# Eight of sixteen gate tiles of a Mamba input projection move into the scan

## Chip, cores and metric

The kernel runs on one core of a Trainium2 chip. The metric is the device time of one execution in microseconds (us), lower is better. Engines are named as the profile names them: PE is the matrix engine, PEld its weight load, DVE the vector engine, ACT the scalar engine, POOL the GpSimd engine, SP the sync engine, which here only issues DMAs. An "ACTq" or "SPq" row is a DMA issued by that engine.

## The reference

One decoder layer on x of shape 2 x 512 x 1024: a Mamba block, a cross attention and a feed-forward, each followed by a residual add and a layer norm. Only the Mamba block is touched by the change:

```
proj = x @ in_proj_w                       # 1024 -> 4096
x, z = split(proj)                         # 2048 channels each; z is the gate
xc   = silu(causal_conv4(x))
dt_r, B, C = rmsnorm of the parts of x_proj(xc)   # 64, 16, 16
dt   = softplus(dt_r @ dt_proj_w.T + dt_bias)
h    = exp(dt * A) * h + dt * B * xc       # per channel and state, 16 states
y    = (sum over states of h * C + D * xc) * silu(z)
out  = y @ out_proj_w.T
```

## The kernel before

The layer is five phases, one after the other. Each phase has its own buffers and semaphores, and the next phase starts when the last has finished. The change touches the first three.

**The input phase** (`mamba_in`, L100) works on tiles of 128 output channels of the projection, for both batch items at once (1024 columns). Tiles 0 to 15 are x, 16 to 31 are z. One tile (`main`, L426) is 8 blocks of the contraction x 2 batch items x 3 passes (`three_passes`, L93: weights and data are split into a high and a low fp32r part, and three products give fp32 accuracy) = 48 matmuls of 512 columns. ACT makes the high part of the next weight tile (L254) and DVE the low part (L332). For an x tile ACT copies the result out (L279), DVE does the four-tap convolution (L358, L363), ACT applies Silu (L281) and PE adds the tile's share of x_proj. The convolved x (`xc`) stays in SBUF for all 32 pairs of tile and batch item, through the scan. For a z tile ACT applies Silu on the way out of PSUM (`gate`, L264) and SP stores it to the DRAM tensor `sz`.

After z tile 17 the 96 rows of x_proj are normalised: PE means (L460), ACT root (L294), DVE reciprocal (L372) and scale (L374, which signals `n_done`). Then the step size dt is made for the 16 channel tiles, two at a time ("a pair"): PE `dt_products` (L470, fp32), ACT Abs and Relu (L302, L303), Exp (L306), Ln (L311), DVE the rest of the softplus (L382, L385, L389, L392, which signals `dt_done`), POOL u = dt * xc (L422). ACT begins a pair's Abs only when DVE has ended the pair before (L298). The loops of L214, L313, L394 and L473 put one pair beside two z tiles, so seven rounds and a tail hold the 14 z tiles from 18 on and eight pairs. SP issues everything in program order: weight load, gate store, weight load, two small dt weight loads, gate store, two dt stores, two u stores (L214 to L226).

**The scan phase** (`mamba_scan`, L483) has 32 blocks (16 channel tiles x 2 batch items), each of NK = 8 steps of two states. Step n of the sequence is

```
POOL dbx(n)  = u * B                        (L732)  128 x 1024
ACT  exp(n)  = exp(dt * A), into PSUM       (L673)  two of 128 x 512
DVE  scan(n), in place in PSUM              (L711)  two of 128 x 512
DVE  g(n-1)  = state * C, PSUM to SBUF      (L701)  128 x 1024
PE   sum(n-1): identity x g, into ps_y      (L758)  two fp32 matmuls
```

The states lie in three PSUM slots (`ps_a`), so exp(n) waits for g(n-3). DVE runs scan(n) half 0, scan(n) half 1, g(n-1). The g buffers are three too, so g(n) waits for sum(n-3). At the start of a block PE adds D * xc with a diagonal matrix (L754) into `ps_y`, for which ACT must have copied out the block before (`after`, L663, placed ahead of the exps of step 4). In blocks 1 to 24, PE also computes the keys of the cross attention with plain fp32 matmuls: 8 chunks of three blocks ("tiles" 0, 1, 2); per block 4 products before the diagonal one and two after each of the steps 0 and 1. ACT copies them out and issues their store at the end of the block, behind the exps of step 7 and ahead of the next block's (`store_keys`, L650). SP brings dt and u two blocks ahead, B and C broadcast to all partitions at the start and at block 16, and the context chunks (L589).

**The output phase** (`project_norm_qkv`, L903) multiplies y by the stored gate on POOL (L1207), splits the product and the output weights into high and low parts (ACT L1066, L1068, DVE L1150, L1152) and runs 32 steps of 24 three-pass products. Three DMAs feed each step: y, gate, weights.

## Time and profile before

| what | us |
|---|---|
| median of 3 runs | 3653.8 |
| lowest, highest | 3651.33, 3656.36 |
| span of the profiled execution | 3652.9 |
| input phase, first instruction to last gate copy | 0 to 424 |
| scan, first DVE scan to last g | 446 to 1309 |
| output phase, the 32 steps | 1326 to 1509 |
| mean granted PE clock, as a share of full speed | 0.972 |

The device time printed for the profiled execution is its span, from the first to the last instruction. Over the whole span the page gives PE 88% busy, DVE 62%, ACT 42%, POOL 34%. Those shares are averages over phases with different limits; each phase is read by itself. A fp32 matmul of 512 columns shows as two records, each with its own PEld record, a fp32r one shows as one.

### The profile page before, as it was taken

The page shows a single profiled execution, that of the slowest core. Times are in us where ns is not written, and L with a number is a line of the kernel's source. Part 1 is how long each engine was busy: PE and PEld are TensorE (multiplying, and loading weights), DVE is VectorE, ACT ScalarE, POOL GpSimd, SP SyncE. Part 2 cuts the span into 40 slices and gives each one's busy share as a digit, 9 for nine tenths or more (in the row PEclk, how much of TensorE's full clock was granted, in tenths as well). Part 3 has the DMA queues.
Part 4 walks back from the last instruction along what each step waited for, and adds up shares of the span by engine and source line. Part 5 has one row for each costly group of instructions (what it writes and reads, how often), then busy time and mean ns, then how long its engine had stood idle before and what let it go on. Part 6 is the DMA issues. An engine that isn't in the chain of part 4 may idle for free. (4 is left out here: it accounts for less than half of the span.)

```text
span 3652.9 us, 41367 instructions
## 1 busy us (share of the span) xinstructions
PE 3225.7 (88%) x12763; PEld 2382.3 (65%) x12763; DVE 2268.0 (62%) x1989; ACT 1518.3 (42%) x2148; POOL 1255.7 (34%) x730
## 2 busy tenths in 40 slices
PE   9999677777776679999799999997889999999996
PEld 7877433333332247888577777776768888888884
DVE  6544499999999956630277777775553233333326
ACT  4457544444444423321177888784231121121111
POOL 0002377667777732100077777772000000000001
PEclk9999799999999999999899999999999999999998
DMA  2124621113111046432211111114211111111101
GB/s 108 40 93 146 223 95 49 45 49 134 45 49 42 20 155 248 158 103 78 93 31 32 33 31 35 31 32 178 93 56 58 35 57 46 40 57 52 36 27 58
DMA packets 125431, 273.18 MB, mean 75 GB/s; under 512 B 24448, under 2 KB 38656, under 8 KB 122400
## 3 DMA queue, kind: packets, MB, share of 16 engines
q1 hardware_dynamic: 107632, 262.42, 21.1%
q10 hardware_dynamic: 17712, 9.79, 0.9%
q8 instruction: 32, 0.52, 0.1%
q14 instruction: 55, 0.45, 0.0%
HBM read 207.87 MB, written 64.29 MB: 75 GB/s over the span
## 5 line engine op out<-in xcount | busy, mean ns | idle before, releaser
L732 POOL TENSOR_TENSOR scan_dbx<-scan_u,scan_b_bc 128x1024 f32<-128x1024 f32 x256 | 602.6, 2355 | 278.4 <-DVE scan_ps_a L711 246.5
L758 PE MATMUL scan_ps_y<-scan_g,scan_ident 128*128 128x512 f32 x1024 | 505.3, 620 | 190.0 <-DVE scan_g L701 190.0
L711 DVE TENSOR_TENSOR_SCAN scan_ps_a<-scan_ps_a,scan_dbx 128x512 f32<-128x512 f32 x512 | 597.0, 1212 | 20.0 <-POOL scan_dbx L732 20.0
L1508 POOL TENSOR_TENSOR at_p_lo<-at_p,at_p_hi 128x512 fp32r<-128x512 f32 x384 | 513.2, 1344 | 176.3 <-ACT at_p_hi L1416 164.0
L673 ACT ACTIVATE scan_ps_a<-scan_dt,scan_a_neg 128x512 f32<-128x512 f32 x512 | 332.8, 682 | 497.4 <-DVE scan_g L701 497.4
L758 PEld LDWEIGHTS scan_ps_y<-scan_g,scan_ident 128*128 128x128 f32 x1024 | 185.7, 194 | 479.7 <-DVE scan_g L701 324.1
L886 POOL TENSOR_TENSOR ff_y<-ff_y,ff_rstd 128x512 f32<-128x512 f32 x14 | 24.9, 1805 | 1126.6 <-DVE ff_rstd L875 1126.6
L1454 DVE TENSOR_REDUCE at_neg_max<-at_ps_mx 128x1 fp32r<-128x1536 f32 x132 | 231.9, 1757 | 174.9 <-PE at_ps_mx L1528 162.4
L701 DVE TENSOR_TENSOR scan_g<-scan_ps_a,scan_c_bc 128x1024 f32<-128x1024 f32 x256 | 308.8, 1207 | 0.0
L1413 ACT ACTIVATE at_p<-at_ps_s 128x512 f32<-128x512 f32 x384 | 228.1, 594 | 116.2 <-PE at_ps_s L1545 96.3
L1928 DVE TENSOR_TENSOR ff_hf<-ff_sg,ff_ps_u 128x1024 f32<-128x1024 f32 x28 | 34.2, 1221 | 388.7 <-PE ff_ps_u L97 388.7
L1416 ACT ACTIVATE at_p_hi<-at_p 128x512 fp32r<-128x512 f32 x384 | 242.8, 632 | 13.2 <-ACT at_p L1413 1.0
L95 PE MATMUL in_ps<-in_x_hi,in_w_hi 128*128 128x512 f32 x512 | 202.5, 396 | 0.0
L96 PE MATMUL in_ps<-in_x_lo,in_w_hi 128*128 128x512 f32 x512 | 201.0, 393 | 0.0
L97 PE MATMUL in_ps<-in_x_hi,in_w_lo 128*128 128x512 f32 x512 | 200.7, 392 | 0.0
L95 PE MATMUL ff_ps_g<-ff_x_hi,ff_w_hi 128*128 128x512 f32 x448 | 176.6, 394 | 5.7 <-DVE ff_x_lo L1868 5.7
L96 PE MATMUL ff_ps_g<-ff_x_lo,ff_w_hi 128*128 128x512 f32 x448 | 175.4, 392 | 0.0
L97 PE MATMUL ff_ps_g<-ff_x_hi,ff_w_lo 128*128 128x512 f32 x448 | 175.3, 391 | 0.0
L95 PE MATMUL ff_ps_u<-ff_x_hi,ff_w_hi 128*128 128x512 f32 x448 | 174.7, 390 | 0.0
L96 PE MATMUL ff_ps_y<-ff_h_lo,ff_w_hi 128*128 128x512 f32 x448 | 174.3, 389 | 0.0
L95 PE MATMUL ff_ps_y<-ff_h_hi,ff_w_hi 128*128 128x512 f32 x448 | 174.3, 389 | 0.0
L96 PE MATMUL ff_ps_u<-ff_x_lo,ff_w_hi 128*128 128x512 f32 x448 | 174.3, 389 | 0.0
(251 smaller groups left out, 6913.9 us busy)
## 6 DMA issues: line engine op xcount, KB each, us to landing
ff_w<-in_w SPq DMA_DIRECT2D x56, 512.0 KB, 4.2
in_w<-in_w_in SPq DMA_DIRECT2D x32, 512.0 KB, 3.5
mid_w<-in_w_out SPq DMA_DIRECT2D x32, 512.0 KB, 4.8
ff_w<-in_w SPq DMA_DIRECT2D x56, 256.0 KB, 2.6
ff_wo_wo<-in_w_o SPq DMA_DIRECT2D x32, 384.0 KB, 3.1
scan_cx<-in_ctx SPq DMA_DIRECT2D x9, 1024.0 KB, 5.6
sz<-in_xz SPq DMA_DIRECT2D x16, 512.0 KB, 3.1
dt<-in_acc SPq DMA_DIRECT2D x16, 512.0 KB, 3.6
```

Source lines behind the costliest of these rows:

```text
L95: nc.tensor.matmul(out, w_hi, x_hi, start=start, stop=False)
L96: nc.tensor.matmul(out, w_hi, x_lo, start=False, stop=False)
L97: return nc.tensor.matmul(out, w_lo, x_hi, start=False, stop=stop)
L673: nc.scalar.activation(ps_a[(2 * s + k) % SB][:, h], dt[s][:], ACT.Exp, scale=a_neg[:, it, 2 * k + h:2 * k + h + 1]).then_inc(a_ready, 1)
L701: nc.vector.tensor_tensor(g[s][:], ps_a[s][:], c_bc[:, 2 * k:2 * k + 2], ALU.mult).then_inc(g_ready, 1)
L711: nc.vector.tensor_tensor_scan(ps_a[slot][:, h], ps_a[slot][:, h], dbx[k % SL][:, h], 0.0, ALU.mult, ALU.add).then_inc(scanned, 1)
L732: nc.gpsimd.tensor_tensor(dbx[k % SL][:], u[s][:].unsqueeze(1).to_broadcast([P, 2, L]), b_bc[:, 2 * k:2 * k + 2], ALU.mult).then_inc(dbx_r ...
L758: last = nc.tensor.matmul(ps_y[:], ident[:], g[(2 * s + k) % SB][:, h], start=False, stop=k == NK - 1 and h == 1)
L1413: nc.scalar.activation(p[t % NSL][:], ps_s[t % 2][:], ACT.Exp, scale=SCALE).then_inc(exp_done, 1)
L1416: nc.scalar.activation(p_hi[t % NSL][:], p[t % NSL][:], ACT.Copy).then_inc(p_hi_done, 1)
L1454: nc.vector.tensor_reduce(neg_max[:, i, HD:HD + 1], ps_mx[:].rearrange("p n l -> p (n l)"), AX_X, ALU.max, negate=True).then_inc(max_done, 1)
L1508: nc.gpsimd.tensor_tensor(p_lo[t % NSL][:], p[t % NSL][:], f32(p_hi[t % NSL][:]), ALU.subtract).then_inc(p_lo_done, 1)
```

## The change

1. z tiles 24 to 31 leave the input phase (ZN = 8). It now has 24 tiles, and `mamba_in` holds one pair of dt tiles beside each z tile from 18 to 23 ("rounds" of two), and two pairs after the last one. z is stored without Silu.
2. The convolved x is stored to DRAM tile by tile (`store_conv`) and read back one block at a time into three buffers by the scan (`load_xc`).
3. The scan computes the eight z tiles. For each chunk of three blocks one z tile is made: 16 plain fp32 products of 512 columns (2 batch items x 8), one after the sum of a step, at the places `Z_STEPS`: steps 2 to 7 of tile 0, 2 to 6 of tile 1, 2 to 6 of tile 2. Batch item 0 is complete after step 3 of tile 1 and batch item 1 after step 6 of tile 2. ACT copies each out and issues its store at the end of that block (`store_gate`), ahead of the next block's exps.
4. The states have two PSUM slots in place of three, and z has two banks: exp(n) waits for g(n-2), and DVE's order becomes scan(n) half 0, g(n-1), scan(n) half 1.
5. The output phase applies Silu to the gate with one more ACT instruction per step, ahead of POOL's multiply.

The core of the diff ("..." where lines are left out):

```diff
+ZN = 8
...
-    NT = 2 * IT
+    NT = 2 * IT - ZN
+    ROUNDS = (NT - IT - 2) // 2
+    assert IT == 4 * ROUNDS + 4
+    xc = nc.alloc_sbuf_tensor_at("xc", [P, B * IT, L], F32, offset=TOP - 4 * B * IT * L)
...
+            def store_conv(m):
+                sp.wait_ge(xc_done, m + 1)
+                sp.dma_start(xc_out[m], xc4[:, :, m, :]).then_inc(xc_st, 16)
...
-            with sp.Fori(0, IT // 2) as j:
-                for s in range(2):
+            next_w(0, 0)
+            next_w(1, 1)
+            with sp.Fori(1, IT // 2) as j:
+                for s in range(2):
+                    store_conv(2 * j + s - 2)
                     next_w(2 * j + s, s)
             for s in range(2):
+                store_conv(IT - 2 + s)
                 next_w(IT + s, s)
                 store_gate(IT + s, s)
...
-            with sp.Fori(IT // 2 + 1, IT - 1) as j:
-                next_w(2 * j, 0)
-                store_gate(2 * j, 0)
-                next_w(2 * j + 1, 1)
-                i = 2 * j - IT - 2
+            def load_dtw(i):
                 for s in range(2):
                     sp.wait_ge(dt_mm, i + s + 1)
                     sp.dma_start(dtw[s][:], d["dt_w"][i + s + 2]).then_inc(dtw_ld[s], 16)
-                store_gate(2 * j + 1, 1)
+
+            def store_pair(i):
                 for s in range(2):
                     store_dt(i + s, s)
                 for s in range(2):
                     store_u(i + s, s)
-            for s in range(2):
...
+            def stores(j, last=False):
+                for s in range(2):
+                    m = IT + 2 + 2 * j + s
+                    load_dtw(4 * j + 2 * s)
+                    if not last:
+                        next_w(m, s)
+                    store_pair(4 * j + 2 * s)
+                    store_gate(m, s)
+
+            with sp.Fori(0, ROUNDS - 1) as j:
+                stores(j)
+            stores(ROUNDS - 1, last=True)
+            load_dtw(IT - 4)
+            store_pair(IT - 4)
+            store_pair(IT - 2)
+            sp.wait_ge(xc_st, 16 * IT)
...
-                act.wait_ge(sz_st[s], 16 * ((m - IT) // 2))
-                nc.scalar.activation(xz[s][:, :, KC - 1:], ps[s][:], ACT.Silu).then_inc(left, 1)
+                act.wait_ge(z_st[s], 16 * ((m - IT) // 2))
+                nc.scalar.activation(xz[s][:, :, KC - 1:], ps[s][:], ACT.Copy).then_inc(left, 1)
...
-            with act.Fori(IT // 2 + 1, IT - 1) as j:
-                next_w(2 * j, 0)
-                gate(2 * j, 0)
-                next_w(2 * j + 1, 1)
-                exponentials(2 * j - IT - 2)
-                logarithms(2 * j - IT - 2)
-                gate(2 * j + 1, 1)
-            next_w(NT - 2, 0)
-            exponentials(IT - 4)
-            logarithms(IT - 4)
-            gate(NT - 2, 0)
-            exponentials(IT - 2)
-            logarithms(IT - 2)
-            gate(NT - 1, 1)
+            def gates(j, last=False):
+                for s in range(2):
+                    m = IT + 2 + 2 * j + s
+                    if not (last and s):
+                        next_w(m, s)
+                    exponentials(4 * j + 2 * s)
+                    logarithms(4 * j + 2 * s)
+                    gate(m, s)
+
+            with act.Fori(0, ROUNDS - 1) as j:
+                gates(j)
+            gates(ROUNDS - 1, last=True)
+            for s in range(2):
+                exponentials(IT - 4 + 2 * s)
+                logarithms(IT - 4 + 2 * s)
...
+            def gates(j, last=False):
+                for s in range(2):
+                    m = IT + 2 + 2 * j + s
+                    if not (last and s):
+                        dve.wait_ge(main_done, m)
+                        split_w(1 - s, m + 2)
+                    softplus(4 * j + 2 * s)
+
+            with dve.Fori(0, ROUNDS - 1) as j:
+                gates(j)
+            gates(ROUNDS - 1, last=True)
             softplus(IT - 4)
...
-            with pe.Fori(IT // 2 + 1, IT - 1) as j:
-                main(2 * j, 0)
-                dt_products(2 * j - IT - 2)
-                main(2 * j + 1, 1)
-
+            with pe.Fori(0, ROUNDS) as j:
+                for s in range(2):
+                    dt_products(4 * j + 2 * s)
+                    main(IT + 2 + 2 * j + s, s)
             for s in range(2):
                 dt_products(IT - 4 + 2 * s)
-                main(NT - 2 + s, s)
...
-    ps_a = [res.bank(f"scan_ps_a{s}", [P, 2, L]) for s in range(SB)]
+    x = sb("x", [P, HT, TOK])
...
+    ps_a = [res.bank(f"scan_ps_a{s}", [P, 2, L]) for s in range(2)]
     ps_y = res.bank("scan_ps_y", [P, L])
-    ps_k = res.bank("scan_ps_k", [P, KC_TOK])
+    ps_k = res.bank("scan_ps_k", [P, L])
+    ps_z = [res.bank(f"scan_ps_z{b}", [P, L]) for b in range(B)]
...
+    Z_STEPS = tuple((s, k) for s, last in zip(range(SB), (8, 7, 7)) for k in range(2, last))
+    assert len(Z_STEPS) == B * HT and ZN == NKC
+    Z_DONE = tuple(Z_STEPS[(b + 1) * HT - 1] for b in range(B))
...
+            def load_xc(it, s):
+                sp.dma_start(xc[s][:], d["xc"][it]).then_inc(xc_ld[s], 16)
+
+            def load_wz(m):
+                sp.dma_start(wz[:], d["w_in"][2 * IT - ZN + m]).then_inc(wz_ld, 16)
...
                 sp.wait_ge(dbx_ready, NK * it)
                 load_u(it + 2, (s + 2) % SB)
                 store(it - 1, (s + 2) % SB)
+                load_xc(it + 2, (s + 2) % SB)
...
             def next_chunk(j):
                 sp.wait_ge(k_mm, KF * j + KF)
                 load_chunk((j + 1) % NKC)
+                sp.wait_ge(z_mm, B * j + B)
+                load_wz((j + 1) % NKC)
...
             load_c(0, 0)
+            load_xc(0, 0)
             load_dt(1, 1)
             load_u(1, 1)
+            load_xc(1, 1)
...
+            load_xc(2, 2)
             sp.dma_start(wk[:], d["w_k"]).then_inc(wk_ld, 16)
             load_chunk(0)
+            load_wz(0)
+            for k in range(HT):
+                sp.dma_start(x[:, k], d["x_t"][k]).then_inc(x_ld, 16)
...
+            def store_gate(m, b):
+
+                act.wait_ge(z_mm, B * m + b + 1)
+                act.wait_ge(z_st[b], 16 * m)
+                nc.scalar.activation(zb[b][:], ps_z[b][:], ACT.Copy).then_inc(zb_done, 1)
+                act.wait_ge(zb_done, B * m + b + 1)
+                act.dma_start(d["z"][b * IT + IT - ZN + m], zb[b][:]).then_inc(z_st[b], 16)
...
-                        nc.scalar.activation(ps_a[(2 * s + k) % SB][:, h], dt[s][:], ACT.Exp,
+                        nc.scalar.activation(ps_a[k % 2][:, h], dt[s][:], ACT.Exp,
                                              scale=a_neg[:, it, 2 * k + h:2 * k + h + 1]).then_inc(a_ready, 1)
...
                     store_keys(chunk, tile)
+                    for b in range(B):
+                        if Z_DONE[b][0] == tile:
+                            store_gate(chunk, b)
...
-                nc.vector.tensor_tensor(g[s][:], ps_a[s][:], c_bc[:, 2 * k:2 * k + 2], ALU.mult).then_inc(g_ready, 1)
+                nc.vector.tensor_tensor(g[s][:], ps_a[k % 2][:], c_bc[:, 2 * k:2 * k + 2], ALU.mult).then_inc(g_ready, 1)
...
                     for h in range(2):
                         dve.wait_ge(a_ready, 2 * n + h + 1)
-                        nc.vector.tensor_tensor_scan(ps_a[slot][:, h], ps_a[slot][:, h], dbx[k % SL][:, h], 0.0,
+                        nc.vector.tensor_tensor_scan(ps_a[k % 2][:, h], ps_a[k % 2][:, h], dbx[k % SL][:, h], 0.0,
                                                      ALU.mult, ALU.add).then_inc(scanned, 1)
-                    if k % 2 == 1:
-                        dve.wait_ge(c_ld[k // 2], 16 * (it // IT + 1))
-                    if not (first and k == 0):
+                        if h or (first and k == 0):
+                            continue
+                        if k % 2 == 1:
+                            dve.wait_ge(c_ld[k // 2], 16 * (it // IT + 1))
                         times_c(n - 1, (slot - 1) % SB, (k - 1) % NK)
-            for free, count in ((scanned, 2 * SL), (g_ready, SB)):
+            for free, count in ((scanned, 2 * SL), (g_ready, 2)):
...
+                def gate_product(i):
+
+                    b, k = divmod(i, HT)
+                    if i == 0:
+                        pe.wait_ge(x_ld, 16 * HT)
+                        pe.wait_ge(wz_ld, 16 * (chunk + 1))
+                    if k == 0:
+                        pe.wait_ge(zb_done, B * chunk + b)
+                    last = nc.tensor.matmul(ps_z[b][:], wz[:, k], x[:, k, b * L:(b + 1) * L], start=k == 0, stop=k == HT - 1)
+                    if k == HT - 1:
+                        last.then_inc(z_mm, 1)
...
                 pe.wait_ge(diag_done, it + 1)
-                nc.tensor.matmul(ps_y[:], d_diag[s][:], xc[:, it], start=True, stop=False)
+                pe.wait_ge(xc_ld[s], 16 * (it // SB + 1))
+                nc.tensor.matmul(ps_y[:], d_diag[s][:], xc[s][:], start=True, stop=False)
                 for k in range(NK):
-                    pe.wait_ge(g_ready, SB + NK * it + k + 1)
+                    pe.wait_ge(g_ready, 2 + NK * it + k + 1)
...
                             last.then_inc(k_mm, 1)
+                    if chunk is not None and (tile, k) in Z_STEPS:
+                        gate_product(Z_STEPS.index((tile, k)))
...
             def step(n, s):
+                act.wait_ge(a_ld[s], 32 * (n // 2 + 1))
+                nc.scalar.activation(gate[s][:], gate[s][:], ACT.Silu).then_inc(silu_done, 1)
                 act.wait_ge(used, n)
...
-                    pool.wait_ge(a_ld[s], 32 * (j + 1))
+                    pool.wait_ge(silu_done, 2 * j + s + 1)
                     nc.gpsimd.tensor_tensor(a[s][:], a[s][:], gate[s][:], ALU.mult).then_inc(gated, 1)
```

## Rows read from the trace of the kernel before

**Rows 1.** Windows: length, busy PE, PEld, DVE, ACT, POOL, clock, DMA share, GB/s
```profile
230.00:426.00 196.00, 190.71 (x743) 140.06 (x741) 97.62 (x81) 142.05 (x130) 43.96 (x14) 0.97 0.42 150
446.00:1309.00 863.00, 611.15 (x1466) 267.83 (x1467) 861.59 (x768) 362.35 (x592) 600.68 (x256) 0.98 0.18 61
```

**Rows 2.** Groups by line, scan: count, busy us, mean ns, idle before and releaser
```profile
L673 ACT ACTIVATE scan_ps_a<-scan_dt,scan_a_neg 128x512 f32<-128x512 f32 x512 | 332.8, 682 | 497.4 <-DVE scan_g L701 497.4
```

**Rows 3.** Timeline of one step of the scan, ACT and DVE: start, length
```profile
602.99 1.21 DVE L701 TENSOR_TENSOR scan_g<-scan_ps_a,scan_c_bc 128x1024 f32<-128x1024 f32 x1
...
604.12 2.33 DVE L711 TENSOR_TENSOR_SCAN scan_ps_a<-scan_ps_a,scan_dbx 128x512 f32<-128x512 f32 x2
...
604.33 1.30 ACT L673 ACTIVATE scan_ps_a<-scan_dt,scan_a_neg 128x512 f32<-128x512 f32 x2 [1.76 <-DVE scan_g L701]
...
606.36 1.21 DVE L701 TENSOR_TENSOR scan_g<-scan_ps_a,scan_c_bc 128x1024 f32<-128x1024 f32 x1
```

**Rows 4.** Timeline, input phase: DVE's last norm step, PE's first two dt products
```profile
240.68 1.28 DVE L374 SCALAR_TENSOR_TENSOR in_pre<-in_acc,in_lnw,in_acc 96x1024 f32<-96x1024 f32 x1
...
243.13 3.70 PE L470 MATMUL in_ps_dt<-in_pre,in_dtw 64*128 64x512 f32 x8
...
268.79 3.70 PE L470 MATMUL in_ps_dt<-in_pre,in_dtw 64*128 64x512 f32 x8
```

**Rows 5.** Windows around an idle PE, columns as in rows 1
```profile
1316.00:1326.00 10.00, 0.00 (x0) 0.00 (x0) 2.91 (x3) 2.98 (x4) 3.31 (x2) 0.50 0.62 210
1326.00:1330.00 4.00, 3.96 (x10) 3.14 (x11) 1.72 (x2) 0.17 (x1) 0.66 (x1) 0.53 0.54 180
```

**Rows 6.** Timeline, input phase: last three pairs, ACT Abs and DVE's last adds
```profile
394.68 1.12 ACT L302 ACTIVATE in_over_ee<-in_ps_dt,in_dt_b 128x1024 f32<-128x1024 f32 x1 [0.97 <-DVE in_acc L392]
...
409.69 1.11 ACT L302 ACTIVATE in_over_ee<-in_ps_dt,in_dt_b 128x1024 f32<-128x1024 f32 x1 [1.92 <-DVE in_acc L392]
...
422.33 2.35 DVE L392 TENSOR_TENSOR in_acc<-in_acc,in_over_rl 128x1024 f32<-128x1024 f32 x2
```

**Rows 7.** Timeline, input phase: SP's weight load, ACT's split of it, two u stores
```profile
294.65 0.37 SPq L179 DMA_DIRECT2D in_w<-in_w_in  x1
...
298.28 1.06 ACT L254 ACTIVATE in_w_hi<-in_w 128x1024 fp32r<-128x1024 f32 x1 [1.31 <-DMA in_w<-in_w_in]
...
411.92 2.71 SPq L212 DMA_DIRECT2D u<-in_under_uu  x2
```

**Rows 8.** Timeline, scan's first steps, POOL: waits for the B broadcasts
```profile
450.31 4.65 POOL L732 TENSOR_TENSOR scan_dbx<-scan_u,scan_b_bc 128x1024 f32<-128x1024 f32 x2 [1.59 <-DMA scan_b_bc<-bc]
455.19 4.66 POOL L732 TENSOR_TENSOR scan_dbx<-scan_u,scan_b_bc 128x1024 f32<-128x1024 f32 x2 [0.23 <-DMA scan_b_bc<-bc]
```

**Rows 9.** Timeline of one block's start, all engines
```profile
607.48 2.33 DVE L711 TENSOR_TENSOR_SCAN scan_ps_a<-scan_ps_a,scan_dbx 128x512 f32<-128x512 f32 x2
...
615.66 0.57 ACT L663 ACTIVATE scan_yb<-scan_ps_y 128x512 f32<-128x512 f32 x1
...
616.47 1.12 PE L754 MATMUL scan_ps_y<-xc,scan_d_diag 128*128 x2 [1.77 <-ACT scan_yb L663]
...
617.43 1.88 PE L758 MATMUL scan_ps_y<-scan_g,scan_ident 128*128 128x512 f32 x4
...
619.14 1.03 PE L742 MATMUL scan_ps_k<-scan_cx,scan_wk 128*128 128x256 f32 x4
...
620.01 1.88 PE L758 MATMUL scan_ps_y<-scan_g,scan_ident 128*128 128x512 f32 x4
```

**Rows 10.** Timeline of one block's end, ACT: key copy and its store's issue
```profile
602.20 0.36 ACT L654 ACTIVATE scan_kb<-scan_ps_k 128x256 f32<-128x256 f32 x1
...
602.73 0.34 ACTq L656 DMA_DIRECT2D k<-scan_kb  x1
```

**Rows 11.** Waits of the output phase, then the table load before Silu, whole kernel
```profile
ACT mid_w_hi L1066 <- DMA mid_w<-in_w_out: 32.9, 7, 10.2
...
L264 ACT ACT_TABLE_LOAD x14 | 18.0, 1283 | 34.2 <-PE in_ps L97 34.1
```

More of the change, by code:

```diff
@@ L150, in mamba_in @@
     w_ld = [sem(f"w_ld{s}") for s in range(2)]
-    sz_st = [sem(f"sz_st{s}") for s in range(2)]
+    z_st = [sem(f"z_st{s}") for s in range(2)]
+    xc_st = sem("xc_st")
     par_ld, bc_st = sem("par_ld"), sem("bc_st")
@@ L513, in mamba_scan @@
     u = [sb(f"u{s}", [P, L]) for s in range(SB)]
+    xc = [sb(f"xc{s}", [P, L]) for s in range(SB)]
     yb = [sb(f"yb{s}", [P, L]) for s in range(SB)]
@@ L522, in mamba_scan @@
     kb = sb("kb", [P, KC_TOK])
-    assert sb.at <= TOP - 4 * NIT * L
-    ps_a = [res.bank(f"scan_ps_a{s}", [P, 2, L]) for s in range(SB)]
+    x = sb("x", [P, HT, TOK])
+    wz = sb("wz", [P, HT, P])
+    zb = [sb(f"zb{b}", [P, L]) for b in range(B)]
+    ps_a = [res.bank(f"scan_ps_a{s}", [P, 2, L]) for s in range(2)]
     ps_y = res.bank("scan_ps_y", [P, L])
-    ps_k = res.bank("scan_ps_k", [P, KC_TOK])
+    ps_k = res.bank("scan_ps_k", [P, L])
+    ps_z = [res.bank(f"scan_ps_z{b}", [P, L]) for b in range(B)]
     par_ld = sem("par_ld")
@@ L533, in mamba_scan @@
     u_ld = [sem(f"u_ld{s}") for s in range(SB)]
+    xc_ld = [sem(f"xc_ld{s}") for s in range(SB)]
+    x_ld, wz_ld, z_mm, zb_done = sem("x_ld"), sem("wz_ld"), sem("z_mm"), sem("zb_done")
+    z_st = [sem(f"z_st{b}") for b in range(B)]
     y_st = [sem(f"y_st{s}") for s in range(SB)]
@@ L605, in next_batch @@
                     if c:
-                        sp.wait_ge(g_ready, SB + last + c * CH // 2)
+                        sp.wait_ge(g_ready, 2 + last + c * CH // 2)
                         load_c(1, c - 1)
@@ L679, in body @@
                     store_keys(chunk, tile)
+                    for b in range(B):
+                        if Z_DONE[b][0] == tile:
+                            store_gate(chunk, b)
             act.dma_start(a_exp[:, 0:IT, :], d["a_log"]).then_inc(par_ld, 16)
@@ L740, in key_product @@
                 def key_product(k):
-                    return nc.tensor.matmul(ps_k[:], wk[:, k, tile * P:(tile + 1) * P], cx[:, k], start=k == 0, stop=k == HT - 1)
+                    return nc.tensor.matmul(ps_k[:, 0:KC_TOK], wk[:, k, tile * P:(tile + 1) * P], cx[:, k], start=k == 0, stop=k == HT - 1)
+                def gate_product(i):
[8 more added lines that the diff above has]
+                        last.then_inc(z_mm, 1)
                 if chunk is not None:
@@ L2062, in phase @@
         res.release()
-    phase(mamba_in, d, xc)
-    phase(mamba_scan, d, xc)
+    phase(mamba_in, d)
+    phase(mamba_scan, d)
     phase(project_norm_qkv, d)
```

39 lines of the change are left out of this document (12 added, 27 removed).

## The prediction, made before any run of the change

> **What bounds the kernel now.** I read the page's slices first (they show the phases), then the windows phase by phase, then the timeline of one step and of the joints between phases. The windows [rows 1] show two phases with different limits. From 230 to 426, where the z tiles and the dt pairs are made, PE is busy 190.7 of 196 us and DVE only 97.6. From 446 to 1309, the scan, DVE is busy 861.6 of 863 us and PE 611.2, so whatever PE does there in DVE's shadow is free, and whatever makes DVE wait is lost. ACT in the scan always waits for g [rows 2]: it has 1.76 us to spare in each step, but that slack exists because exp is one slot ahead. One step of DVE is 606.36 - 602.99 = 3.37 us: g, then 1.12 us per scan half, each starting when the one before it ends [rows 3].
>
> **Input phase.** The normalised dt rows are ready at 240.68 + 1.28 = 242.0 [rows 4]. Nothing of the change moves that. Two dt products are 3.7 us, and between their starts at 243.13 and 268.79 lie they and two z tiles, so a z tile is (25.66 - 3.7) / 2 = 11.0 us [rows 4]. After: the first products no longer wait for z tile 18 and start at 242.0. PE will have been idle some ten us by then. After 10 idle us and more before the output phase it ran its first 4 us at 0.53 of full speed, the 1.2 GHz level [rows 5]; I take that, so the first tile's products need 3.6 us, not 1.85, and ACT's first Abs is at 245.5 (at full clock 243.8).
>
> From there the pairs are a chain: Abs, Relu, Exp, Ln on ACT, then DVE, whose end lets ACT begin the next. At the end of the phase this chain ran bare: Abs at 394.68 and 409.69, last DVE add over at 422.33 + 2.35 = 424.7, so 15.0 us a pair [rows 6]. One round of the new loop is one pair and one z tile: PE 3.7 + 11.0 = 14.7 us, just under the chain. In it ACT also makes a weight split (1.06) and a copy; the copy was in the 15.0 already, with a table load of 1.28 that goes, as Silu goes. ACT waited 1.92 us before the Abs of 409.69 [rows 6], so the split fits. DVE's split falls in the time in which it waits for Exp. SP is in order: its u stores ended at 411.92 + 2.71 = 414.6, 5 us after a pair's end; then come gate store, two dt weights (2.2 us together) and the next weight load, whose data ACT uses 298.28 - 294.65 = 3.6 us later [rows 7]. That is 11 to 12 us after the pair's end and is wanted at about 13.5. So eight pairs take 8 x 15.0 = 120.1 us, the last ends at 365.6 in place of 424.7: **-59.1 us**. Bounds: -60.8 with a warm PE; -47 if each of six rounds takes 2 us more because a weight is late. The 16 stores of xc (512 KB each) and their waits in SP's queue cost nothing: each waits for a Silu that precedes the weight split that SP waits for anyway. The phase's tail keeps its order.
>
> **Start of the scan.** Two xc loads of 256 KB stand ahead of the second B broadcast, for which POOL already waits 1.59 us. B and C chunks arrive 2 MB per 455.19 - 450.31 = 4.9 us [rows 8], so 0.5 MB is **+1.2 us**. The 4 MB of x and 0.5 MB of z weights queue behind everything that the first block needs; at that rate they have landed 11 us after the context chunk, some 10 us into block 1, before its step 2. Cost nothing; bound +5.
>
> **The z products in the scan.** A sum of four records takes 619.14 - 617.43 = 1.71 us, four key records 620.01 - 619.14 = 0.87 [rows 9]. A z product is two 512-column records, 0.86 us; a step then asks PE for 1.71 + 0.86 = 2.57 of 3.37 us. PE has the room, but it starts each block late. Before, the diagonal product began 616.47 - 607.48 = 9.0 us into the block [rows 9], because ACT's copy of the previous block stands behind the exps of step 3, which wait for g(0). With two slots they wait for g(1). In the new order g(1) begins 2 x 3.37 + 1.12 = 7.86 us into the block where g(0) began 5.61 in: 2.25 later. So the diagonal starts at 11.2, and PE works without a gap: 0.96, three sums 5.13, keys 1.74, then five z products 4.30 and four sums 6.84. The last z product of tile 2 (behind step 6) ends at 11.2 + 19.0 = 30.2 us, while DVE wants to begin the next block at 8 x 3.37 = 27.0. The sums themselves are in time for the three g buffers.
>
> **ACT's wait for it** is the price of the change. `store_gate` stands ahead of the next block's exps in ACT's program. It waits for 30.2, then: result visible 0.2, copy 0.6, 0.2 to the DMA issue, issue 0.35 (key copy and its issue [rows 10]), then the first exp 0.68 [rows 2] and 0.15 to DVE: 32.4. DVE stands 5.4 us, with nothing else to do. Queued behind ACT's wait are both exps of step 0, hence DVE, hence g(7), PE's last sum and the next block's keys; SP's z weights and context wait too, with a block to spare. In tile 1 the same code finds its result ready (step 3 was long ago): key copy, issue, z copy, issue end 25.9 us into the block, and the next exps are due at 26.05. There PE waits 1.2 us for that copy, which its slack holds. One stall per chunk, 8 x 5.4 = **+43.4 us**. Bounds: nothing, if PE were ready in time, and 8 x 8 = 64.
>
> **Two slots.** exp(n) half 0 now starts 1.34 us after g(n-2) starts [rows 3], that is 2.46 us into step n-1, takes 0.68 and is needed at 3.37: 0.23 us for the hand-over. The nearest hand-overs are 0.13 us (DVE's g over at 604.20, exp at 604.33 [rows 3]) and 0.24 (ACT's copy over at 616.23, PE at 616.47 [rows 9]). I take nothing; the bound from 0.24 is 0.01 x 256 = 3 us.
>
> **Batch change at block 16.** Two B and two C broadcasts now wait behind the z products (SP's wait before the weight load), to about 30.2 us into block 15, and come 2 MB per 4.9 us from there. B for step 4 lands 3 to 4 us into the delayed block 16, when POOL, three steps ahead, asks for it; C for step 2 by 7, wanted at 7.9 or later. Nothing; bound +5.
>
> **Output phase.** ACT gets a Silu per step (0.68, as a 512-column exp) and, once in a loop pass, a table load of 1.28 [rows 11]. It comes when the gate has landed, ahead of the wait for PE, and a step of PE is 5.4 us, so mostly it hides. In six of 32 steps ACT waited for the weights' DMA, up to some us (seven waits, the longest being the phase's start [rows 11]); there up to 1.96 us can show. Between 0 and 12 I take **+1.5**. The Trainium skill, ScalarE: Activation LUTs, section What ACT_TABLE_LOAD costs, gives the load as about 1.28 us, which the row confirms, but adds a drain of about 1.38 us to every switch; by an estimate from that page a late step would cost 3.3 us and this term at most 20.
>
> **Sum.** -59.1 + 1.2 + 43.4 + 1.5 = -13.0. The profiled execution took 3652.9 us, so 3639.9; its time is 0.9 below the median of 3653.8, well inside the runs' spread. I say 3640. A measurement of this kernel can tell about 0.2% (7.3 us) from no change.
>
> **Rivals.**
> *A. The slots bind (slower).* If the hand-over of exp half 0 to DVE's scan overruns its 0.23 us, every step pays, since g, exp and scan then form a ring with DVE idle in it. For it: the margin is less than one of the hand-overs shown, and waits in loops carry register work. Against it: ACT sits ready in each step. Overrun of 0.1 us a step: 256 x 0.1 = 25.6, giving 3665.5. It takes the gain from 13.0 / 256 = 0.05 us on and is clearly slower from 0.08.
> *B. No stall at the chunk's end.* If PE gets through in time, the +43.4 vanish: 3596.5. For it: PE has spare time in sum. Against it: it would have to gain 5 us after a start that ACT's order fixes.
> *C. The input phase gives less.* If the late weight (in the old loop ACT waited 1.31 us for one [rows 7]) adds 2 us to six rounds, or the output phase shows its Silus, 12 us go: 3652, no change.
>
> **Chances.** My forecast 0.57, with its own range 3630 to 3650 (stall 4.5 to 6.5 us); A 0.15; B 0.13; C 0.15. Below 3646.5: 0.47 of the forecast and all of B. Within 0.2%: the forecast's rest, most of C, some of A: 0.22. Above 3661: 0.18, A and pile-ups of the small bounds. The range 3610 to 3667 leaves out B's full size and A beyond 0.1 us a step.
>
> **What would show it.** Abs pitch of 15.0 us through the input phase and last dt add near 365.6. In the scan a DVE idle of about 5.4 us, 8 times, before the first scan of a block, released by ACT's exp; the steps between still 3.37; the diagonal product 11.2 us into a block. ACT's z copies of batch item 1 waiting for PE, those of item 0 not. The forecast is wrong if DVE also idles a little in every step (A), if there are no long idles (B), or if the Abs pitch is over 16 (C).

## The result and the profile after

The changed kernel takes 3689.9 us (median of 4 runs, 3687.5 to 3701.9) against 3654.3 for the kernel before: 1.0106 times as long, 95% interval 1.0092 to 1.012. The forecast was 3640, with a range of 3610 to 3667. The profiled execution has a span of 3689.3 us, 36.4 more than before, and a mean granted clock of 0.945 in place of 0.972.

The input phase did nearly what was forecast. Timeline of the kernel after: both of ACT's Abs of the first pair, then the first Abs of the second pair and of the last two; DVE's last dt add and its first scan. The last two Abs and the dt add answer to [rows 6].

```profile
245.69 1.11 ACT L316 ACTIVATE in_over_ee<-in_ps_dt,in_dt_b 128x1024 f32<-128x1024 f32 x1 [9.76 <-PE in_ps_dt L489]
249.10 1.11 ACT L316 ACTIVATE in_over_ee<-in_ps_dt,in_dt_b 128x1024 f32<-128x1024 f32 x1 [1.29 <-PE in_ps_dt L489]
264.35 1.11 ACT L316 ACTIVATE in_over_ee<-in_ps_dt,in_dt_b 128x1024 f32<-128x1024 f32 x1
...
339.37 1.11 ACT L316 ACTIVATE in_over_ee<-in_ps_dt,in_dt_b 128x1024 f32<-128x1024 f32 x1 [2.13 <-DVE in_acc L407]
354.39 1.11 ACT L316 ACTIVATE in_over_ee<-in_ps_dt,in_dt_b 128x1024 f32<-128x1024 f32 x1 [4.26 <-DVE in_acc L407]
...
367.01 2.35 DVE L407 TENSOR_TENSOR in_acc<-in_acc,in_over_rl 128x1024 f32<-128x1024 f32 x2
...
389.85 3.53 DVE L768 TENSOR_TENSOR_SCAN scan_ps_a<-scan_ps_a,scan_dbx 128x512 f32<-128x512 f32 x3 [18.21 <-POOL scan_dbx L790]
```

The pitch of the last pairs is 354.39 - 339.37 = 15.0 us, but the first round took 264.35 - 245.69 = 18.7. (The two behind it took 16.2 and 13.75, together as long as two of 15.0.) The phase ends at 367.01 + 2.35 = 369.4, which is 55.3 us earlier than before. DVE's first scan is at 389.85 in place of 446.46: 56.6 us gained.

All of that and more is lost in the scan. First the windows of the kernel after, over the scan and the output phase (columns as in [rows 1]), then all that DVE waited for between 385 and 1350: us in total, times, longest.

```profile
390.00:1350.00 960.00, 756.70 (x1724) 353.97 (x1724) 865.74 (x768) 373.05 (x610) 598.69 (x255) 0.89 0.22 77
1364.00:1592.00 228.00, 220.40 (x1005) 186.08 (x1006) 132.94 (x136) 100.61 (x127) 50.27 (x31) 0.99 0.62 217
```

```profile
DVE scan_ps_a L768 <- ACT scan_ps_a L727: 50.4, 8, 6.7
DVE scan_g L758 <- PE scan_ps_y L829: 41.2, 27, 2.2
DVE scan_ps_a L768 <- POOL scan_dbx L790: 19.9, 2, 18.2
```

The first row is the stall at the end of a chunk, forecast at 43.4. The second was not forecast at all: 27 times the g of a block's step 3 waits for one of PE's sums. The third is the scan's start, 20.0 us before the change too. From DVE's first scan to its last g the scan takes 960.9 us in place of 862.1. The two waits make 91.6 of these 98.8. DVE's own busy time grows by 4 to 5 (865.7 in the window against 861.6), since two of its instructions overlap by some 0.1 us (604.12 against 604.20 in [rows 3]) only where no wait lies between them. PE's clock in the window fell from 0.98 to 0.89.

One chunk's end and the block behind it show both waits (timeline of the kernel after, start and length):

```profile
595.61 1.88 PE L829 MATMUL scan_ps_y<-scan_g,scan_ident 128*128 128x512 f32 x4
597.32 1.02 PE L810 MATMUL scan_ps_z<-scan_x,scan_wz 128*128 128x512 f32 x2
598.38 0.60 ACT L709 ACTIVATE scan_zb<-scan_ps_z 128x512 f32<-128x512 f32 x1 [6.22 <-PE scan_ps_z L810]
599.14 0.34 ACTq L711 DMA_DIRECT2D z<-scan_zb  x1
600.16 1.30 ACT L727 ACTIVATE scan_ps_a<-scan_dt,scan_a_neg 128x512 f32<-128x512 f32 x2 [1.18 <-issue]
600.88 1.23 DVE L768 TENSOR_TENSOR_SCAN scan_ps_a<-scan_ps_a,scan_dbx 128x512 f32<-128x512 f32 x1 [5.95 <-ACT scan_ps_a L727]
...
603.28 3.78 PE L829 MATMUL scan_ps_y<-scan_g,scan_ident 128*128 128x512 f32 x4 [4.93 <-DVE scan_g L758]
...
611.33 0.57 ACT L717 ACTIVATE scan_yb<-scan_ps_y 128x512 f32<-128x512 f32 x1
...
612.17 2.07 PE L825 MATMUL scan_ps_y<-scan_xc,scan_d_diag 128*128 128x512 f32 x2 [2.54 <-ACT scan_yb L717]
...
614.03 2.59 PE L829 MATMUL scan_ps_y<-scan_g,scan_ident 128*128 128x512 f32 x4
...
616.73 1.22 DVE L758 TENSOR_TENSOR scan_g<-scan_ps_a,scan_c_bc 128x1024 f32<-128x1024 f32 x1 [1.16 <-PE scan_ps_y L829]
```

Two things are to be seen. First, ACT stands 6.22 us for the last z product and DVE 5.95 behind it, as forecast. Second, the diagonal product begins 612.17 - 600.88 = 11.3 us into the block, as forecast, but it takes 2.07 us where it took 1.12 before [rows 9], and the sum behind it 2.59 for 1.88. PE had idled twice by then (4.93 and 2.54 us), and the granted clock from 612 to 616 is 0.57: most of that stretch was at the lower of its two levels (1.2 GHz). The g of the block's step 3 needs the buffer that this first sum reads, so it has to wait for the sum.

The output phase is shorter: from DVE's first split in it to the end of the last of its v sums it takes 228.6 us after and 232.1 before. ACT now mostly finds the weights there, and waits for the gates instead. Waits of the output phase, kernel after; the last row answers to [rows 11], where it was 32.9 us.

```profile
ACT mid_gate L1139 <- DMA mid_gate<-z: 24.0, 16, 4.4
ACT mid_w_hi L1142 <- DMA mid_w<-in_w_out: 5.3, 6, 2.3
```

### The profile page after: what moved, and what is told of

Read it like the earlier page. It is cut to its first block and busy times, and to the rows that moved or that the text cites. A ratio compares the mean times of both kernels' runs of the same rounds, so it can differ in the third digit from the quotient of the medians.

```text
span 3689.3 us, 41228 instructions
## 1 busy us (share of the span) xinstructions
PE 3281.5 (89%) x12635; PEld 2396.5 (65%) x12635; DVE 2252.5 (61%) x1981; ACT 1508.2 (41%) x2163; POOL 1249.5 (34%) x730
## 5 line engine op out<-in xcount | busy, mean ns | idle before, releaser
L768 DVE TENSOR_TENSOR_SCAN scan_ps_a<-scan_ps_a,scan_dbx 128x512 f32<-128x512 f32 x512 | 599.1, 1213 | 71.2 <-ACT scan_ps_a L727 50.4
L829 PE MATMUL scan_ps_y<-scan_g,scan_ident 128*128 128x512 f32 x1024 | 529.7, 648 | 75.9 <-DVE scan_g L758 75.9
L829 PEld LDWEIGHTS scan_ps_y<-scan_g,scan_ident 128*128 128x128 f32 x1024 | 211.7, 210 | 349.1 <-issue 231.6
L758 DVE TENSOR_TENSOR scan_g<-scan_ps_a,scan_c_bc 128x1024 f32<-128x1024 f32 x256 | 309.3, 1208 | 41.3 <-PE scan_ps_y L829 41.2
L1489 ACT ACTIVATE at_p<-at_ps_s 128x512 f32<-128x512 f32 x384 | 228.1, 594 | 118.6 <-PE at_ps_s L1621 98.8
L825 PE MATMUL scan_ps_y<-scan_xc,scan_d_diag 128*128 128x512 f32 x64 | 60.1, 1039 | 154.9 <-ACT scan_yb L717 120.4
L98 PE MATMUL ff_ps_y<-ff_h_hi,ff_w_lo 128*128 128x512 f32 x448 | 174.5, 390 | 0.0
L98 PE MATMUL ff_ps_u<-ff_x_hi,ff_w_lo 128*128 128x512 f32 x448 | 174.5, 390 | 0.0
```

The source lines that it names most:

```text
L98: return nc.tensor.matmul(out, w_lo, x_hi, start=False, stop=stop)
L758: nc.vector.tensor_tensor(g[s][:], ps_a[k % 2][:], c_bc[:, 2 * k:2 * k + 2], ALU.mult).then_inc(g_ready, 1)
L768: nc.vector.tensor_tensor_scan(ps_a[k % 2][:, h], ps_a[k % 2][:, h], dbx[k % SL][:, h], 0.0, ALU.mult, ALU.add).then_inc(scanned, 1)
L829: last = nc.tensor.matmul(ps_y[:], ident[:], g[(2 * s + k) % SB][:, h], start=False, stop=k == NK - 1 and h == 1)
L1489: nc.scalar.activation(p[t % NSL][:], ps_s[t % 2][:], ACT.Exp, scale=SCALE).then_inc(exp_done, 1)
```

## Theories

*Theory.* Two separate things cost the change its gain. (1) ACT runs its program in order, and `store_gate` for the second batch item stands ahead of the next block's exponentials. (2) The two slots tie the exponentials of step 3 to g(1), where three slots tied them to g(0). The copy of the finished block stands behind them, and so the diagonal product comes 2.3 us later in the block, while the last sum ahead of it comes 1.1 us sooner (g has moved ahead of the second scan half). PE idles one step, 3.4 us, longer than before, its clock falls, and the first sum is late.

*Rivals.* The z products fill PE, and whatever waits for PE waits for that load. Or it is the lateness alone that costs, or the clock alone. Or the hand-over of two slots costs a little in every step.

## Experiments

In every ratio the kernel before ran on the same chip; where the chips differ, ratios are to be compared.

### The slot order alone

```
-ps_a = [res.bank(f"scan_ps_a{s}", [P, 2, L]) for s in range(SB)]
+ps_a = [res.bank(f"scan_ps_a{s}", [P, 2, L]) for s in range(2)]
...
-for free, count in ((scanned, 2 * SL), (g_ready, SB)):
+for free, count in ((scanned, 2 * SL), (g_ready, 2)):
```

(with g in DVE's program between the scan halves and the other counts, as in the change)

> The kernel before with two slots for the states in place of three, and nothing else of the change. Theory (late copy, cold PE): the exponentials of step 3 now wait for g(1), so the copy of the finished block, and with it the diagonal product, comes 3.4 us later than with g(0); PE stands 5 us or more at each block's start, runs the diagonal and the first sum at 0.5 of full clock, and g(3) of the block waits for that sum. In the trace of after the eight blocks without any key or z product show such a wait of 0.77 to 2.19 us, 1.5 in the mean, and the whole scan 41.2 us of it. So 31 x 1.3 = 41 us: about 3695, DVE waiting for PE some 25 to 31 times in the scan. Rival (z products): PE is late because of the z products it has to do; without them the two slots cost nothing: 3654, no waits of g for PE.

3706.8 us, 1.0146 of before (1.0129 to 1.0163). The one wait of DVE that is new, then one block's start:

```profile
DVE scan_g L701 <- PE scan_ps_y L759: 50.1, 31, 2.2
```

```profile
599.23 2.07 PE L755 MATMUL scan_ps_y<-xc,scan_d_diag 128*128 x2 [5.14 <-ACT scan_yb L663]
...
601.10 3.05 PE L759 MATMUL scan_ps_y<-scan_g,scan_ident 128*128 128x512 f32 x4
...
604.26 1.23 DVE L701 TENSOR_TENSOR scan_g<-scan_ps_a,scan_c_bc 128x1024 f32<-128x1024 f32 x1 [1.59 <-PE scan_ps_y L759]
```

Without one z product in the scan, all 31 blocks behind the first have the wait, the seven without keys too. The slot order costs 53.6 us by itself, some 1.7 us a block. The rival that PE's load makes it is out. In the changed kernel the wait is shorter (41.2 us, 27 times): in most blocks with z products PE idles some 3.1 us there, not 5.14, and the four blocks without the wait are those in which the diagonal product took 1.12 us, at full clock.

### The slot order with the block copy one step earlier

```
-if k == 4 and not (isinstance(it, int) and it == 0):
+if k == 3 and not (isinstance(it, int) and it == 0):
     after(it - 1, (s - 1) % SB)
```

> The kernel before with two slots and with the block copy one step earlier. Theory: two slots cost nothing of themselves, only through the place of the copy, which now again stands behind exponentials that wait for g(0): 3654, within 4 us, no waits of g for PE. Rival (the hand-over of the slots costs a little in each step): above 3660, and the run with two slots alone would hold that part too.

3653.2 us, 1.0001 of before (0.9991 to 1.001). All the 53.6 us are back with one line moved. The diagonal product of a block with keys, then of one without:

```profile
589.48 1.12 PE L755 MATMUL scan_ps_y<-xc,scan_d_diag 128*128 x2 [1.77 <-ACT scan_yb L663]
...
1208.58 2.07 PE L755 MATMUL scan_ps_y<-xc,scan_d_diag 128*128 x2 [3.52 <-ACT scan_yb L663]
```

PE idles 1.77 us, not 5.14, and the product takes 1.12 us, not 2.07. Two slots cost nothing in a step; that rival is out. The second row says more. In the blocks without keys PE idles 3.5 us even with the early copy (and in the kernel before), and four of these blocks ran the diagonal product at half clock, with first sums of up to 3.62 us. No g waited for PE in any of them. So half clock alone, with the product in time, costs nothing.

### PE kept busy while it waits

These runs add throw-away products to the changed kernel, ahead of the keys and the diagonal product of a block. The first used 14 of them in a block with keys and 30 in one without:

> The kernel after with throw-away products on PE (14 of 256 columns ahead of the keys of a block, 30 in blocks without keys) while it waits for ACT's copy of the finished block; they are written where the key products go and are overwritten. The diagonal product starts as late as in after; only the clock differs. Theory (the clock is what makes the late start dear): diagonal product at 1.0 in place of 2.07 us, first sum at 1.9 in place of 3.6, and the waits of g for PE (41.2 us) go; stall at the chunk's end 5.4 in place of 6.3 us: 3690 - 41 - 7 = 3642. Rival (lateness alone): g waits as before, 3690.

3744.7 us, 1.0246 of before (1.0229 to 1.0263): slower by far. The products were too many. A product of 256 columns takes 0.43 us, twice what I had counted, and the throw-away ones pushed the keys and the diagonal product back: g waited 92.6 us for PE, up to 6.8 at a time. This run says nothing about the clock. With 5 and 12:

```
+for _ in range(5 if chunk is not None else 12):
+    nc.tensor.matmul(ps_k[:, 0:KC_TOK], ident[:], wk[:, 0, 0:KC_TOK], start=True, stop=True)
```

> As the run before with throw-away products, but so few that they end before ACT's copy of the finished block: a product of 256 columns took 0.43 us there (two records), so 14 were 6 us long and pushed the keys and the diagonal product themselves back. Now 5 (2.2 us, in a gap of 3.1) and 12 in blocks without keys (5.2 us, in a gap of 6.9). Theory (cold PE): diagonal product 1.0 us, the waits of g for PE (41.2 us) go and the chunk's stall shrinks by up to 1 us: 3690 - 41 - 7 = 3642. Rival (lateness alone is what is paid): 3690, g waits as in after.

3647.0 us, 0.9987 of before (0.9977 to 0.9996). Waits of DVE in the scan, and PE's wait before the diagonal product:

```profile
DVE scan_ps_a L768 <- ACT scan_ps_a L727: 47.6, 8, 6.0
DVE scan_ps_a L768 <- POOL scan_dbx L790: 18.6, 2, 16.9
...
PE scan_ps_y L833 <- ACT scan_yb L717: 39.3, 30, 3.0
```

The wait of g for PE is down from 41.2 us to 1.2, once, in the first block that has it. ACT's copy comes where it came in the changed kernel, and the diagonal product still waits for it, but takes 0.66 us a record in place of 1.04. So the late copy at full clock costs g next to nothing, and half clock without the late copy cost nothing either: it takes both. 43 us come back; the traces put 40.0 to the waits of g and 2.8 to the stall. The late copy keeps a smaller price of its own, in the stall at the chunk's end: 47.6 us here, 35.8 with the copy early (below), and that run is 12 us faster.

The Trainium skill, TensorE: Matmul & The Clock Gate, section HAM oscillation — how this bites in real kernels, describes a PE that idles for DMA in each turn of a loop and so starts each turn cold. The runs agree in kind: with two slots alone PE idles 5.14 us in each block with keys and then takes 2.07 us for 1.12. Here an in-order copy on ACT makes the gaps, and most of the price is not PE's own time but DVE's.

### The store moved behind the next block's exponentials

```
+if k == 3 and late:
+    store_gate(chunk - 1, 1)
...
-for b in range(B):
-    if Z_DONE[b][0] == tile:
-        store_gate(chunk, b)
+if Z_DONE[0][0] == tile:
+    store_gate(chunk, 0)
```

> The kernel after with the copy and store of the second batch item's z tile moved in ACT's program from the end of a chunk to behind the exponentials of step 2 of the next block (seven of the eight times; the last stays where it was). Theory (ACT's order makes the stall): seven stalls of 6.3 us go, 44 us: 3646; the waits of g for PE stay, since PE still starts each block late. Rival (PE's backlog is what is paid, whoever waits): the stall turns into longer waits of g for PE in the same block and the time stays within 10 us of 3690.

3654.0 us, 1.0002 of before (0.9992 to 1.0011): 36 us faster than the changed kernel, where 44 were expected. In the trace the scan is 40.7 us shorter; the difference lies behind the scan, where traces of the changed kernel and its versions scatter by 5 us.

```profile
DVE scan_g L769 <- PE scan_ps_y L840: 43.4, 27, 2.2
...
DVE scan_ps_a L779 <- ACT scan_ps_a L729: 5.6, 1, 5.6
DVE scan_g L769 <- DMA scan_c_bc<-bc: 2.8, 1, 2.8
```

Seven of eight stalls are gone (50.4 to 5.6), and the waits of g grew by 2.2 us only (41.2 to 43.4): PE's backlog, what it still has to do when a chunk ends, need not be paid by anyone. One wait of 2.8 us for C appeared at the change of batch item; the loads of C stand behind the z products in SP's queue, and the forecast had a bound of 5 for it.

### The block copy early in the changed kernel

> The kernel after with ACT's copy of the finished block one step earlier, ahead of the exponentials of step 3 and so behind those of step 2, which wait for g(0). Theory: the diagonal product begins 3.37 us earlier in the block (7.8 in place of 11.2), PE no longer idles long there and stays at full clock; the waits of g for PE (41.2 us) go, and the stall at the chunk's end (50.4 us) shrinks by 8 x 3.4 = 27 us and by what half clock added: 3690 - 41 - 34 = 3615. Rival (z products alone make PE late): only the stall shrinks by 27: 3663, and g still waits for PE about 25 times.

3635.0 us, 0.9949 of before (0.9933 to 0.9966), 55 us faster than the changed kernel; 75 were expected. The waits of g for PE are gone. The stall shrank less than it should:

```profile
DVE scan_ps_a L768 <- ACT scan_ps_a L727: 35.8, 9, 4.9
PE scan_ps_z L810 <- ACT scan_zb L709: 35.3, 8, 4.4
```

The second row looks like the reason. PE's first product of the second batch item waits 4.4 us for ACT's copy of the *first* item, because one semaphore counts both copies. So that was set right next:

```
-pe.wait_ge(zb_done, B * chunk + b)
+pe.wait_ge(zb_done, B * chunk)
```

> The kernel after with the copy of the finished block one step earlier, as before, and with PE's wait before the second batch item's products set to what it needs, the copy of the previous chunk's tile: one semaphore counts both items' copies, and the wait as it stands also asks for this chunk's first item, which ACT copies only at the end of tile 1. In the run with the early copy alone PE stood 35.3 us there (8 times), and DVE still stood 35.8 us at the chunk ends. Theory: PE gives that wait back at once, so the last z product ends 3.4 us or more sooner and the stall falls from 4.4 to 1 to 2 us: 3635 - 8 x 2.5 to 3.4 = 3608 to 3615. Rival: PE is full of work by then, the wait only moves: 3635.

3634.2 us, 0.9951 (0.9934 to 0.9968). A miss: PE's wait is gone, and the time is the same. The timeline of a chunk's end says why:

```profile
495.23 1.20 DVE L758 TENSOR_TENSOR scan_g<-scan_ps_a,scan_c_bc 128x1024 f32<-128x1024 f32 x1
...
496.49 1.98 PE L829 MATMUL scan_ps_y<-scan_g,scan_ident 128*128 128x512 f32 x4 [0.52 <-DVE scan_g L758]
...
498.31 1.02 PE L810 MATMUL scan_ps_z<-scan_x,scan_wz 128*128 128x512 f32 x2
499.37 0.60 ACT L709 ACTIVATE scan_zb<-scan_ps_z 128x512 f32<-128x512 f32 x1 [4.57 <-PE scan_ps_z L810]
...
501.88 1.23 DVE L768 TENSOR_TENSOR_SCAN scan_ps_a<-scan_ps_a,scan_dbx 128x512 f32<-128x512 f32 x1 [4.31 <-ACT scan_ps_a L727]
```

PE has caught up: it waits 0.52 us for g. But the last z product stands behind the sum of step 6 in PE's program, and DVE makes g(6) only within step 7. So it can't be over before the block is, however fast PE is. Its place in the order gives a floor of 4.3 us a chunk. (The run before had already reached it: six of its eight stalls are 4.2 to 4.3 us.)

### The last z product one and two steps earlier

```
-for s, last in zip(range(SB), (8, 7, 7)) for k in range(2, last)
+for s, last in zip(range(SB), (8, 8, 6)) for k in range(2, last)
```

> The run with the early copy and PE's wait set right, and in it the z products one place forward: the last stands behind the sum of step 5 of tile 2, not of step 6. That run missed its forecast: PE had caught up, and yet DVE stood 34.3 us at the chunk ends, 4.3 each. In its trace the last z product waits for the sum of step 6, whose g DVE makes within step 7, so it can't end before the block does: a floor set by its place in PE's order. Theory (floor by place): one step earlier is 3.37 us sooner, the stall is 4.3 - 3.4 = 0.9 us, 8 times: 3634 - 27 = 3607. Rival (PE's load sets it): one product per step more in tile 1 changes nothing, 3634.

3605.6 us, 0.9886 of before (0.987 to 0.9903). 27 us were expected to go. The chip is another one, on which the kernel before ran 5 us faster, so the times are not to be subtracted: against before on its own chip this run gains 42 us and the last one 19. In the traces the scan is 26.8 us shorter.

```profile
DVE scan_ps_a L768 <- ACT scan_ps_a L727: 7.4, 8, 1.0
```

The stall is 0.9 us a chunk, 3.4 less than 4.3: the floor moves with the place. One step further forward:

> The same with the last z product behind the sum of step 4 of tile 2 (tile 1 takes seven, from its step 1 on). Theory (floor by place): no stall is left, though ACT's store stands where the change put it, at the end of the chunk: 3596, as the run in which the store was moved. Rival: step 1 of tile 1 now asks PE for a sum, keys and a z product (3.44 of 3.37 us) and tile 1 has no slack, so g waits for PE: 3605 or more.

3602.4 us, 0.9877 (0.9861 to 0.9894); 3596 was expected.

```profile
DVE scan_ps_a L768 <- ACT scan_ps_a L727: 3.1, 8, 0.4
```

The product is long done, and ACT's z copy waits for nothing of PE's, but 0.4 us a chunk stay: two copies and two DMA issues in a row stand ahead of the exponentials. g never waits for PE, so the fuller tile 1 costs nothing visible. By ratio this version is some 10 us behind the next one, but its scan is only 4.4 us longer; what makes the rest is open.

### All three put in order

Copy early, each wait for a z copy as long as it has to be, and the second item's store behind the exponentials of step 5 of the next block, all eight times:

> The kernel after with three things in order: block copy one step earlier; each of PE's waits for a z copy asks only for the copy that it needs; the second item's z copy and store stand in ACT's program behind the exponentials of step 5 of the next block, all eight times. Theory: no stall at chunk ends and no waits of g for PE; what is left of the change is the shorter input phase and what little the output phase and the start give: 3635 - 36 = 3599, DVE standing only at the scan's start. Rival (PE's backlog has to be paid somewhere in the scan): 3615 or more, with waits of g for PE.

3595.3 us, 0.9846 of before (0.9829 to 0.9862), faster than both kernels. In a later run:

> The fastest version so far once more, so that the one beside it is compared on the same chip: 0.985 of the time before, and 18.5 to 19 us between the first Abs of the first and of the second pair.

3597.8 us, 0.9848 (0.9834 to 0.9861). The window of its scan, columns as in [rows 1], and the only wait of DVE in it:

```profile
390.00:1256.00 866.00, 715.72 (x1724) 318.93 (x1724) 862.66 (x768) 372.39 (x610) 599.97 (x256) 0.98 0.25 86
```

```profile
DVE scan_ps_a L781 <- POOL scan_dbx L803: 20.6, 2, 18.9
```

The scan is 865.2 us long from DVE's first scan to its last g, 3.1 more than before, and PE does the z products in it at 0.98 of its clock, 716 us busy for 611. What is left of the change is nearly all its input phase.

### PE kept busy in the input phase

```
 last.then_inc(ms_done, 1)
+for w in range(40):
+    nc.tensor.matmul(ps_xp[:, w % B], zero[:, 0:E], x_hi[:, 0, 0:L], start=True, stop=True)
```

> The fastest version so far (block copy early, each wait for a z copy as long as needed, the second item's store late) with 40 throw-away products on PE in the 10 us in which it waits for the normalised dt rows in the input phase, written to a bank whose result has been read. In after the first dt products ran at half clock (the eight records 7.2 us for 3.7), as did the z tile behind them, and the first pair took 18.7 us where later ones took 15.0. Theory (cold PE made the first round longer): first Abs 1.7 us sooner, the second round 15.0 to 15.5 us behind it, and the whole phase 3.5 to 5 us shorter: 3595 - 4 = 3591. Rival (the first round is long for the table loads and splits on ACT): only the first Abs moves, 1.7 us, and the pitch stays 18.7.

3595.1 us, 0.9843 (0.9829 to 0.9856), beside 3597.8 without the throw-away products: 2.7 us less, in the direction expected but not more than these runs scatter. The trace is clearer. PE's dt products and ACT's Abs of the first and the second pair, in this run:

```profile
242.02 3.69 PE L491 MATMUL in_ps_dt<-in_pre,in_dtw 64*128 64x512 f32 x8 [0.82 <-DVE in_pre L389]
...
244.13 1.11 ACT L316 ACTIVATE in_over_ee<-in_ps_dt,in_dt_b 128x1024 f32<-128x1024 f32 x1 [7.95 <-PE in_ps_dt L491]
...
258.90 1.11 ACT L316 ACTIVATE in_over_ee<-in_ps_dt,in_dt_b 128x1024 f32<-128x1024 f32 x1
```

and the products in the same run's neighbour without the throw-away ones:

```profile
241.94 7.18 PE L489 MATMUL in_ps_dt<-in_pre,in_dtw 64*128 64x512 f32 x8 [9.97 <-DVE in_pre L389]
```

The first round is 14.8 us long, not 18.8 as in that neighbour, and the pairs stay 5.7 us ahead from there on. PE at its lower clock was what made it long.

## Why the prediction was wrong

The sign was wrong through one price: the waits of g for PE, which the prediction put at nothing. It priced the hand-over of a slot under **Two slots** (a margin of 0.23 us a step, nothing lost), and that was right: steps are still 3.37 us, and with the copy put back the slots cost 0. It also worked out, two parts earlier, that the slot order delays the diagonal product to 11.2 us into the block (11.3 measured), and used this only for the z products. The step that failed is there. "PE works without a gap: 0.96, three sums 5.13" took full clock after an idle PE, and "The sums themselves are in time for the three g buffers" followed from it. At full clock this is true (the run with 5 and 12 throw-away products). At half clock the diagonal product and the first sum took up to 2.07 + 3.62 us, and g waited up to 2.2. Priced 0, this costs 41.2 us in the changed kernel and 53.6 alone. The rows for it were in hand: [rows 5] shows PE at 0.53 of its clock after an idle, and the prediction charged that to the input phase's first products. I did not ask the same of a gap that the change itself opens in each block.

From the forecast of -13.0 to the +36.4 us of the profiled execution: input phase +3.8, start of the scan -2.5, stall +7.0, waits of g +41.2, lost overlap and small waits of the scan +7.2, everything behind the scan -7.3.

The other steps:

- **Input phase**, forecast -59.1, measured -55.3. The chain of 15.0 us a pair held from the second round on (the second and third in sum). The first products' half clock was charged at 1.8 us, once, but it held for all eight records (7.19 us) and part of the z tile behind them, and cost 5.7 us in all. With PE kept busy the gain comes to its bound of -60.8. Late weights (rival C) did not show, and the 16 stores of xc cost nothing visible.
- **Start of the scan**, forecast +1.2: the stretch from the last dt add to the first scan came out 1.3 us shorter. It scatters by 2 to 3 us between runs (first scans at 387.97 and 390.81 in two of one kernel). The x loads landed in time.
- **ACT's wait**, forecast 43.4, measured 50.4: 6.3 each for 5.4. In the chunk shown PE's last z product ended 3.4 us after the block (3.2 forecast), and from there to DVE took 2.5 us (2.2 forecast), since 0.7 us lie between the end of the DMA issue and the next exponential. What is left of the 6.3 is PE's half clock (5.95 in the run with 5 and 12 throw-away products). Taken away at seven chunks of eight, the stall gave 36 us.
- **Tile 1**: PE waited 0.85 us for the first item's copy (6.8 us in 8 waits), 1.2 forecast, and its slack held it. With the copy early, this wait grows to 4.4 and still costs nothing, because the last product's place sets the end.
- **Batch change**: 0, as forecast; 2.8 us once the stalls ahead of it were taken away.
- **Output phase**, forecast +1.5, measured some -3 (232.1 to 228.6 us; 227.4 to 230.4 in the other traces with the Silus, 231.4 and 231.8 in those without): the Silus fit into ACT's waits. Why the phase got shorter is not shown. The Trainium skill, ScalarE: Activation LUTs, section What ACT_TABLE_LOAD costs, adds about 1.38 us of drain to a table load. No run here shows it: in the input phase Exp ends at 253.11, the load runs from 253.13 for 1.28 us and Ln begins at 254.42.

Of the rivals, A came nearest in size (3665.5) and had the right culprit and the wrong mechanism: it put the loss into each step's hand-over, and the traces put it once in a block, through the copy's place and the clock. B, no stall, was priced at 3596.5, and the version in which both waits are gone takes 3595.3. That is partly luck: its input phase gains 4 us less than was priced and its scan is 3 us longer, while the start of the scan and what lies behind it gain more.

## What to carry to other kernels

When a change takes a buffer away, find what stands *behind* the longer wait in an in-order engine's program: here one copy came a step later, and moving one line was worth 53.6 us. A gap that a change opens on PE has to be priced with the half clock behind it, and by who waits for PE's first result and how soon, even where PE has slack on average. And an operation's end has a floor from its place in its engine's order; where two waits cover each other (PE's for the copy, ACT's for the product), removing the visible one may give nothing.

## What was not expected of the hardware

- A gap of a few us was enough for the lower clock level. In the 24 blocks with keys PE idled 1.77 us before the diagonal product in the kernel before and with two slots and the early copy, and the product took 1.12 us each time. With two slots alone it idled 5.14 and the product took 2.07 each time. In between both are found: after 3.1 us in the changed kernel 1.12 at 579.19 and 2.07 at 640.36; after 3.51 us in the blocks without keys of the kernel before 1.12 at 1208.65 and 2.07 at 1235.56. So such a gap isn't safe, and its price varies from block to block.
- Throw-away products on PE pay: 5 to 12 in a block brought 43 us. The count has to stay under the gap: 14 to 30 cost 55 us.
- A store at the end of a loop's body delays what follows it a little. Between the issue of the second item's z store and the exponential behind it lie 0.66 to 0.69 us (599.48 to 600.16), seven times. The DMA issue is not the reason: behind the first item's store, within the same loop's body, the exponential follows after 0.34 (474.16 to 474.50). What the trace has more at the loop's end is an ALU instruction and a branch in ACT's program.
